# Decoder layer: expert_w applied to the latents in the feed-forward part instead of to fc2_w, and x2's transposes moved up in stage one's end

## The reference, cut to what matters

```
x = layernorm(x + attention(x, Wq, Wk, Wv))                 # 1024 tokens x 1024
x = layernorm(x + fake_quant(x) @ fake_quant(ctx))          # "cross"
# feed-forward, hidden = x
logits = hidden @ gate_w                                     # 8 experts
r      = sum(top_k(logits, 2))                               # one number a token
shared = relu(hidden @ up_w) ** 2 @ down_w                   # 1024 -> 2048 -> 1024
latent = hidden @ fc1_w                                      # 1024 -> 512
routed = ((latent @ expert_w) * r) @ fc2_w                   # 512 -> 512 -> 1024
x = layernorm(x + layernorm(shared + routed, ln_gamma, ln_beta))
```

## Time and profile before

| | us |
|---|---|
| median of 3 runs | 710.58 (708.35 to 712.87) |
| the profiled execution | 706.96 |
| its span, first to last instruction | 705.2 |
| start of stage one's end (its last projected tile is done) to the last x2 store | 178.6 to 251.3 |
| feature products | 262.1 to 490.3 |
| phases | 493.4 to the norms' end at 705 |

### The profile page before, as it was taken

The page is one execution under the profiler, slowest core; times in us unless marked ns, Lnnn a source line. Parts: engine busy times, 40 slices in busy tenths (PEclk is TensorE's granted clock), DMA queues, the critical chain, the costliest instruction groups (busy, mean ns, idle before and its releaser), DMA issues.

```text
span 705.2 us, 7841 instructions
## 1 busy us (share of the span) xinstructions
PE 620.1 (88%) x2952; PEld 501.4 (71%) x2960; DVE 415.0 (59%) x552; ACT 292.9 (42%) x378; POOL 137.9 (20%) x162
## 2 busy tenths in 40 slices
PE   4598699887559879989999999998999999999972
PEld 3487577765348548868888888886888888888862
DVE  6846788997888523222334222132875555769976
ACT  4545555556363524222233323203254433434825
POOL 3424283555730411313110000000000000000000
PEclk9999999998878999999999999999999999999987
DMA  9654335433761469684884825500433235352402
GB/s 337 226 170 152 112 108 169 131 92 102 244 198 39 145 203 316 207 293 149 263 304 149 273 107 158 171 8 1 122 113 94 89 91 201 126 210 61 148 31 119
DMA packets 80887, 109.88 MB, mean 156 GB/s; under 512 B 23633, under 2 KB 54609, under 8 KB 80849
## 3 DMA queue, kind: packets, MB, share of 16 engines
q1 hardware_dynamic: 76096, 92.07, 40.6%
q0 software_dynamic: 2448, 8.91, 3.6%
q10 hardware_dynamic: 2304, 8.39, 3.5%
HBM read 79.99 MB, written 25.17 MB: 149 GB/s over the span
## 4 chain that ended last, share of the span: by engine, by line
PE 58%; DVE 21%; DMA 7%; issue 5%; ACT 4%; SPq 4%; POOL 2%; POOLq 0%; DVEq 0%; ACTq 0%
PE acc_b L1172 31%; PE acc_a L1201 13%; PE acc_b L1201 8%; DMA c_sb<-in_ctx_dram 2%; SPq L243 1%; SPq L235 1%; DVE stat L571 1%; DMA x_scratch<-res 1%; PE qkv_ps L283 1%; PE sc_ps L300 1%; DVE o_sb L615 1%; ACT y_sb L425 1%; DVE x2T_hi L1457 1%; PE xa_ps L325 1%; DVE stat_n L1508 1%
## 5 line engine op out<-in xcount | busy, mean ns | idle before, releaser
L1388 DVE TENSOR_TENSOR u_lo<-u_raw,u_hi 128x1024 fp32r<-128x1024 f32 x18 | 23.3, 1293 | 123.1 <-ACT u_hi L1244 123.1
L1172 PE MATMUL acc_b<-x2T_hi,u_hi 128*128 128x512 f32 x160 | 63.3, 396 | 0.0
L1172 PE MATMUL acc_b<-x1T_hi,u_hi 128*128 128x512 f32 x160 | 62.4, 390 | 0.0
L1172 PE MATMUL acc_b<-x2T_hi,u_lo 128*128 128x512 f32 x160 | 62.4, 390 | 0.0
L1172 PE MATMUL acc_b<-x2T_lo,u_hi 128*128 128x512 f32 x160 | 62.3, 390 | 0.0
L1172 PE MATMUL acc_b<-x1T_hi,u_lo 128*128 128x512 f32 x160 | 62.3, 389 | 0.0
L1172 PE MATMUL acc_b<-x1T_lo,u_hi 128*128 128x512 f32 x160 | 62.3, 389 | 0.0
L283 PE MATMUL qkv_ps<-w_hi,xT_hi 128*128 128x512 f32 (+1 forms) x128 | 35.9, 362 | 14.7 <-DVE w_lo L642 10.0
L1201 PE MATMUL acc_a<-x2T_lo,x2T_hi 128*128 128x512 f32 x168 | 41.8, 404 | 3.8 <-DVE x2T_lo L1459 3.8
L1201 PE MATMUL acc_a<-x1T_hi,x2T_hi 128*128 128x512 f32 x168 | 41.1, 399 | 3.0 <-DVE x1T_hi L1459 3.0
L1201 PEld LDWEIGHTS acc_a<-x2T_lo,x2T_hi 128*128 128x128 f32 x168 | 32.9, 197 | 11.7 <-issue 4.6
(11 more groups left out here) (235 smaller groups left out, 1346.1 us busy)
## 6 DMA issues: line engine op xcount, KB each, us to landing
d_raw<-in_L_ffn_down_w_dram SPq DMA_DIRECT2D x28, 512.0 KB, 5.5
t_scratch<-d_raw SPq DMA_DIRECT2D x20, 512.0 KB, 4.2
d_raw<-t_scratch SPq DMA_DIRECT2D x20, 512.0 KB, 3.8
c_sb<-in_ctx_dram ACTq DMA_DIRECT2D x16, 512.0 KB, 4.7
u_raw<-in_L_ffn_up_w_dram SPq DMA_DIRECT2D x16, 512.0 KB, 6.6
x_sb<-in_x_dram SPq DMA_DIRECT2D x8, 512.0 KB, 4.7
res<-in_x_dram SPq DMA_DIRECT2D x8, 512.0 KB, 3.4
x_scratch<-res SPq DMA_DIRECT2D x8, 512.0 KB, 3.6
```

The source lines that it names most:

```text
L1172: mm = pe.matmul(acc_b[:, q % 4], s, v, start=(k == 0 and i == 0), stop=(k == KT - 1 and i == 2))
L1388: dve.tensor_tensor(u_lo[:, m % 2], u_raw[:, m % 2], u_hi[:, m % 2].bitcast(F32), ALU.subtract).then_inc(S["u_lo_done"], 1)
```

## The change

- expert_w is no longer multiplied by fc2_w. All of the w2 work of stage one goes: loads, transposes, splits, the 8 products, copies, stores, the scratch.
- Part two makes the latents first (4 blocks of fc1_w by 2 batches). ACT and DVE split each product into high and low parts. expert_w is loaded by SP behind the column loads and gamma, and split. Eight expert products (expert_product, 4 row blocks by 2 batches, 4 x 3 matmuls each) follow, and DVE multiplies them by rT. Then come the 16 up blocks. The last pair of feature blocks in the phases is the expert output, and its rows of the second operand are fc2_w itself.
- The routing and spreading steps come earlier, between the latent products. down_w's sums follow another timetable (SUMS_AT), with their stores two blocks later. rT, gamma, beta, ones and r_diag get storage of their own; the features are laid out in three parts each.
- In stage one x2's column blocks get eight buffers instead of four, all eight are loaded in step 8, and all eight transposes stand in PE's list in step 8: 0 and 1 ahead of values(6), 2 to 7 behind it and ahead of scores(7). On DVE x2T_lo 0 to 3 stand ahead of first_stats(5), 4 and 5 ahead of normalise(5), 6 and 7 ahead of collect(6). On ACT softmax_exp(7) stands ahead of q1T_out(5).
- The first two weight blocks that stage one loads and splits are of fc1_w.
- Code for making some up products already in stage one (early_product and its like) is there but off: EARLY = 0.

The diff, cut to its core:

```diff
+EARLY = 0
...
-                if k >= 4:
-                    sp.wait_ge(S["x2T_ready"], k - 3)
-                sp.dma_start(xk[k % 4], x2_dram[0:SEQ, k * P:(k + 1) * P].rearrange("(t p) c -> p t c", p=P)).then_inc(xk_in[k % 4], 16)
+                    sp.wait_ge(S["c_done"], BATCH * CK)
+                sp.dma_start(xk[k], x2_dram[0:SEQ, k * P:(k + 1) * P].rearrange("(t p) c -> p t c", p=P)).then_inc(xk_in[k], 16)
...
-                if s == TILES - 1:
-
-                    sp.wait_ge(S["scores_ready"], TILES - 1)
-                    for l in range(MT):
-                        sp.dma_start(ex_raw[l], args["expert_w"][l * P:(l + 1) * P, :]).then_inc(ex_in, 16)
-                    sp.wait_ge(S["xT_ready"], TILES)
-                    sp.wait_ge(S["c_done"], BATCH * CK)
-                    for m in range(MT):
-                        sp.dma_start(fc2_raw[m], args["fc2_w"][m * P:(m + 1) * P, :]).then_inc(fc2_in[m], 16)
-                if s == TILES + 3:
-                    store_w2(range(MT - 1))
...
                 if s == TILES:
-                    transpose_expert(0)
-                    transpose_expert(1)
-                if s == TILES + 1:
-                    transpose_x2(4)
-                    transpose_x2(5)
+                    transpose_x2(0)
+                    transpose_x2(1)
                 if in_range(s - 2):
                     values(s - 2)
                 if s == TILES:
-                    transpose_expert(2)
-                    transpose_expert(3)
-                    transpose_x2(0)
-                    transpose_x2(1)
-                if s == TILES + 1:
-                    transpose_x2(6)
-                    transpose_x2(7)
+                    for k in range(2, KT):
+                        transpose_x2(k)
...
-                for q in w2_ahead.get(s, ()):
-                    w2_product(q)
...
                 if s == TILES + 1:
-                    fc2_lo_out(0)
-                    fc2_lo_out(1)
                     softmax_transpose(s - 2)
-                    x2T_lo_out(4)
-                    x2T_lo_out(5)
-                    fc2_lo_out(2)
-                    fc2_lo_out(3)
                     collect(s - 2)
-                    x2T_lo_out(6)
-                    x2T_lo_out(7)
...
                 if s == TILES:
                     softmax_transpose(s - 2)
-                if s == TILES:
-                    expert_lo(0)
-                    expert_lo(1)
+                    for k in range(4):
+                        x2T_lo_out(k)
                 if s in (TILES, TILES + 1):
                     first_stats(s - 3)
...
+                if s == TILES:
+                    x2T_lo_out(4)
+                    x2T_lo_out(5)
...
                 if s == TILES:
+                    x2T_lo_out(6)
+                    x2T_lo_out(7)
                     collect(s - 2)
...
+            def expert_product(e, b):
+
+                q = expert_index(e, b)
+                bank_free(q)
+                pe.wait_ge(S["ex_lo_done"], 2)
+                for l in range(MT):
+                    pe.wait_ge(S["lat_lo_done"], latent_index(l, b) + 1)
+                    st = [x[:, l, e * P:(e + 1) * P] for x in (ex_hi, ex_lo)]
+                    for i, (s, v) in enumerate(split_products(st, [lat[l][b][:, h] for h in range(2)])):
+                        mm = pe.matmul(acc_b[:, q % 4], s, v, start=(l == 0 and i == 0), stop=(l == MT - 1 and i == 2))
                 mm.then_inc(S["op_used"], 1)
...
             routing(0)
+            latent_product(0, 0)
+            transpose_logits(0)
+            latent_product(1, 0)
+            latent_product(0, 1)
+            spread_r(0)
+            latent_product(1, 1)
+            routing(1)
+            latent_product(2, 0)
+            transpose_logits(1)
+            latent_product(2, 1)
+            latent_product(3, 0)
+            spread_r(1)
+            latent_product(3, 1)
             for b in range(BATCH):
-                for m in range(2):
-                    product(m, b)
-                    if (m, b) == (0, 0):
-                        transpose_logits(0)
-            for m in range(2, MU):
-                for b in range(BATCH):
-                    product(m, b)
-                if m == 2:
-                    spread_r(0)
-                if m == 3:
-                    routing(1)
-                if m == 4:
-                    transpose_logits(1)
-                if m == 6:
-                    spread_r(1)
+                for e in range(MT):
+                    expert_product(e, b)
+            for m in range(MU):
+                if m >= EARLY:
+                    up_product(m, 0)
+                up_product(m, 1)
```

More of the change, by code:

```diff
@@ L91, in attention_and_cross @@
         q1T = sb("q1T", [P, 2, KT, P], BF16)
[L92 to L95, removed]
+        q2 = sb("q2", [P, BATCH, CK, EMB], BF16)
         c_sb = sb("c_sb", [P, 2, EMB], F32)
@@ L753, in _ @@
                     magic(s - 3)
+                    for m in range(5, min(6, EARLY)):
+                        early_lo(m)
                 if in_range(s - 4):
@@ L940, in feed_forward, with two_types, h_pair, h_slot @@
         xT_hi, xT_lo = [so["x2T_hi"], x1_hi], [so["x2T_lo"], x1_lo]
-        f1b0, f2b0, f1b1, f2b1 = [sb(n, [P, NP, SEQ], F32) for n in ("f1b0", "f2b0", "f1b1", "f2b1")]
-        h_block = lambda m, b: ((f1b0, f1b1), (f2b0, f2b1))[m % 2][b][:, m // 2]
+        def two_types(name, slots):
+            with nc.sbuf_tensor(name + "_r", [P, slots, SEQ], F32R) as rounded:
+                pass
+            return rounded, sb(name, [P, slots, SEQ], F32)
+        ex_hi, h_a1 = two_types("h_a1", 4)
+        ex_lo, h_a2 = two_types("h_a2", 4)
+        lat_st, h_b = zip(*[two_types(f"h_b{i}", 4) for i in range(4)])
+        h_c = [sb(f"h_c{i}", [P, 2, SEQ], F32) for i in range(4)]
+        part_of = [(so["hx1"][:, KT:KT + 4], h_b[0], h_c[0]), (so["hx2"][:, KT:KT + 4], h_b[1], h_c[1]), (h_a1, h_b[2], h_c[2]), (h_a2, h_b[3], h_c[3])]
+        def h_pair(half, b, j):
+            part = part_of[2 * b + half][j // 2]
+            return part[:, 2 * (j % 2):2 * (j % 2) + 2]
+        def h_slot(half, b, k):
+            return h_pair(half, b, k // 2)[:, k % 2]
+        lat = [[lat_st[2 * b + l // 2][:, 2 * (l % 2):2 * (l % 2) + 2] for b in range(BATCH)] for l in range(MT)]
         s3_own = sb("s3_own", [P, 2, SEQ], F32)
@@ L989, in feed_forward, with u_src @@
         up_cols, fc1_cols = [args[w].rearrange("(k p) (m c) -> m p k c", p=P, c=P) for w in ("up_w", "fc1_w")]
-        def u_src(m):
-            half, j = m % 2, m // 2
-            return up_cols[half * UP + j] if j < UP else fc1_cols[half * (NP - UP) + j - UP]
+        def u_src(w):
+            return fc1_cols[w] if w < MT else up_cols[(w - MT) % 2 * UP + (w - MT) // 2]
         def d_rows(half, k, tiles=1):
             return args["down_w"][(half * UP + k) * P:(half * UP + k + tiles) * P] if k < UP else \
-                w2_dram[(half * (NP - UP) + k - UP) * P:(half * (NP - UP) + k - UP + tiles) * P]
+                args["fc2_w"][(half * (NP - UP) + k - UP) * P:(half * (NP - UP) + k - UP + tiles) * P]
         t_rows = lambda half, k, tiles=1: t_dram[half][k * P:(k + tiles) * P, :]
@@ L1026, in a_raw @@
         def a_raw(phase, j):
-            return s3_of(j) if phase == "p7" else pair({"p1": f1b0, "p6": f1b0, "p5": f1b1, "p4": f2b1, "p3": f1b0, "p2": f2b0}[phase], j)
+            return s3_of(j) if phase == "p7" else h_pair(*{"p1": (0, 0), "p6": (0, 0), "p5": (0, 1), "p4": (1, 1), "p3": (0, 0), "p2": (1, 0)}[phase], j)
         def consumed(eng, s):
```

462 lines of the change are left out of this document (256 added, 206 removed).

## The result

| | before | after |
|---|---|---|
| median, the four runs of each made together, us | 709.47 (706.85 to 712.87) | 729.79 (729.32 to 731.50) |
| ratio | | 1.0288, 95% interval 1.0238 to 1.0338 |
| the profiled execution; its span | 706.96; 705.2 | 731.5; 729.7 |
| TensorE's first matmul of part two | 253.62 | 259.45 |
| start of p1 | 493.40 | 520.26 |

Differences between profiles are therefore read stage by stage here. Three points of TensorE's own list cut the 24.5 us into stages: part two starts 5.8 us later, the stretch from there to p1 is 21.0 us longer (260.8 against 239.8), and what follows p1's start is 2.4 us shorter (209.4 against 211.8).

A forecast was written before the change was run, and what follows sets the result against it. TensorE was taken to bound the feature products, a chain through all engines stage one's end. +21.8 - 2.6 + 1.7 + 2.0 = +22.9 us, from the median 710.58 giving 733.5; forecast 733, range 722 to 741.

The forecast's parts named there:

- The matmuls, +21.8: Feature products: 96 added expert matmuls at 0.227 us each, with nothing to cover them, lengthen the kernel by 21.8 us.
- the wait for rT, -2.6: Feature products: TensorE's 2.63 us idle before the routing of batch 1 goes, -2.6 us.
- The start of p1, +1.7: Hand-over from feature products to p1: TensorE's wait grows from 3.14 to 4.8 us, +1.7.
- Stage one's end, +2.0: End of stage one: earlier loads offset by moved transposes, then slow-clock crosses; both halves together +2.0 us.
- The first half: Stage one's end up to normalise(6): moved transposes take what the dropped split gave, +0.2 us, normalise(6) near 225.2.
- the clock of cross(7): Second half of stage one's end: slow clock after idle TensorE, 1.9 us charged for this cross, likewise for cross(6).
- The second half: Stage one's end from normalise(6) to part two's opening: clock charges less two small gains, sum +2.3 us.
- The term for values(7): First half of stage one's end: values(7) follows cross(5) closely and takes 2.0 us instead of 3.78, gaining 1.8.
- 0.8 off for transpose_q1(7): Second half of stage one's end: this transpose no longer stands behind the w2 products, -0.8 us.
- The 0.7 for the landing: Opening of part two: the last landing is x2's at 254.9, not w2's at 255.6, -0.7 us.
- stage one's end becomes clearly shorter: Rival on stage one's end: 9 us come off through less VectorE work and earlier transposes, 722 us; chance 0.13.
- PE's clock stays low: Rival on stage one's end: crosses 5, 6, 7 each 3.4 us dearer, +29 in all, 740 us; chance 0.12.

The follow-up runs named there:

- experiment 1: Kernel before with each of the 8 w2 products cut from 12 matmuls to 1: 712.45 us, ratio to before 1.0023.
- 2: Kernel after with each of the 8 expert products cut from 12 matmuls to 1: 716.81 us, ratio to before 1.0116.
- experiment 4: Kernel after with p1's first three high parts ahead of the last relu on ScalarE: 724.11 us, ratio to before 1.0201.
- experiment 9: Kernel before with the low parts of p1's first pair ahead of the last latent on VectorE: 702.83 us, ratio to before 0.9921.
- experiment 3: Kernel after with x2's transposes and splits in the order of before, early loads and eight buffers kept: 723.97 us, ratio to before 1.0207.
- run 7: Kernel after with x2's order of before, p1's first splits early and filler matmuls (40, 12 and 24): 712.95 us, ratio to before 1.0086.
- 10: Kernel after with x2's order of before and p1's first splits early, no filler matmuls: 718.50 us, ratio to before 1.0124.
- 5: Kernel after with 102 filler matmuls that feed nothing in TensorE's pauses of stage one's end: 728.57 us, ratio to before 1.0282.
- 8: Kernel after with EARLY = 8 and p1's first splits ahead of the last relu: 725.97 us, ratio to before 1.0247.
- 6: Kernel after with EARLY = 8, eight up products made in stage one: 734.48 us, ratio to before 1.0359.
- run 11: Kernel before with p1's first low parts moved up and p3's last low parts ahead of four tiles' statistics: 702.68 us, ratio to before 0.9910.

## Why the prediction was right, and where its terms were off

733 was forecast with 722 to 741, and slower with 0.94; 729.8 came. +22.9 was predicted; the medians give +20.3, the profiles +24.5. That 729.8 lies so near 733 is in part luck: stage one's end was taken 3.8 us too short, and a tail that came out 2.4 us shorter by chance made up for most of it. Stage by stage, profile against profile:

- **The matmuls, +21.8, and the wait for rT, -2.6: right.** Together +19.2 against the measured +19.4. Experiments 1 and 2 show both sides: 20 us of w2 matmuls were worth nothing where they lay, the expert matmuls are on the path where they are. Inside the 19.4 are small terms that I had not listed. Part two now opens at the low clock: its 16 routing matmuls need 2.4 us more (6.1 against 3.7), behind a pause of 7.70 us where before, with the last w2 product behind cross(7), it was 2.77. The wait of before for the loads of x2's second batch, 1.3 us, is gone. With them the sum makes 20.3; the 0.9 us by which the stretch is shorter than that I can't place.
- **The start of p1, +1.7: right.** The wait is 4.78 us, +1.6; experiment 4 removes it and finds the place of all of it in ScalarE's list. I did not say what experiment 9 shows, that the 3.14 us of before were a loss of 5 us to be had by moving two instructions.
- **Stage one's end, +2.0: the mechanism right, the size not.** It is +5.8. The first half (+2.4 and not +0.2) and the clock of cross(7) (+2.8 and not +1.9) were mis-sized. The second half as a whole came to +3.5, where I had +2.3, and laying both halves out together had taken another 0.5 off.
  - In the first half I put softmax_max(7) at 206.4; it is 208.3. I took the column loads as 1.04 us apart, and the second came 2.1 us behind the first. I also took scores(7) with 2.9 us; it stands behind a pause of 5.37 us and took 3.75. My +0.2 is +2.4 (normalise(6) at 227.37, forecast 225.2). The term for values(7) held: 1.95 us, forecast 2.0.
  - In the second half I charged 1.9 us of low clock for each cross. cross(6) lost 1.8 (5.46 against 3.63), but cross(7) lost 2.8. The 1.9 came from p1's burst of 24 matmuls, whose clock came back within the burst; behind cross(6) TensorE paused again for 4.43 us, and in cross(7) the clock came back later.
  - I took 0.8 off for transpose_q1(7), and that held: before, it started 0.9 us behind its input (239.06, 239.97), now 0.06 (243.49, 243.55). The 0.7 for the landing is 0.5 up to TensorE's first matmul of part two (257.59 to 259.45, before 251.30 to 253.62). The loads behind the last store start 1.7 us sooner after it (2.7 against 4.4), but that first matmul doesn't wait for them; they count in the next stage, as the 1.3 us of wait that is gone there. In all 2.4 + 1.8 + 2.8 - 0.8 - 0.5 = 5.7, of 5.8 measured.
- **The tail, which I took as unchanged, is 2.4 us shorter**, by chance and not by the change (below).

The rival "stage one's end becomes clearly shorter" asked the right question: the end could have been shorter. With the transposes left where they were, part two starts 6.8 us earlier than in after (experiment 3), and with fillers as well 12.5 us earlier (run 7, 246.90 against 259.45). The moved transposes took the gain away, as the sum said. The rival "PE's clock stays low" was half true: the slow level held cross(5) as well, 5.63 us where it had been at the full clock. Little of these 2.0 us came through, since values(7) gave back 1.8 behind it. The Trainium skill ("Perfetto Trace Analysis", Matmul Optimizations) advises back-to-back matmuls because the engine's power follows its use. The trace agrees in the direction: 0.70 against 0.88 as the clock of the stretch, with 37.5 against 55.0 us of TensorE's work in it.

From the kernel after, by the ratios to before, experiments take off 5.7 us (the order, 3), 6.2 (the start of p1, 4) and 2.7 (the pauses left empty, 10 against 7; by itself not clear of noise, 4.7 in the traces), and at run 7 some 6 us to the kernel before are left. By the profiled executions of run 7 and before these are +18.4 for the feature products without the wait at their end (255.0 against 236.6), -6.7 for the earlier start of part two, and the 3.1 of wait, 1.7 of slow start and 1.1 of tail that run 7 is spared. Since the hand-over to p1 can be mended in the kernel before as well (run 9), the like comparison is run 7 with run 9, 1.0086 with 0.9921: the change costs 1.7%, some 12 us (8 to 15), even with its side effects mended.

What stays open: how much of the 4.7 and 5.9 us that the fillers gave at the start of part two (7 against 10, and 5) reaches the time of the whole kernel, which the intervals of 5 us and more don't tell; and the 0.9 us above.

## What to carry to other kernels

An operation's cost is set by where it stands: 96 matmuls in the gaps of a chain bound by other engines cost nothing, the same 96 in a stretch where TensorE is full cost 21.8 us, and taking them back out of there would return only what the next engine's own chain leaves (12 to 13 of 20 us). Before work is moved up in an in-order list, ask what stands behind it: eight transposes ahead of scores(7) made the chain wait for work that nobody needed until part two. And look at the hand-over between stages first; moving one pair of low parts ahead of one multiply gave 5.4 us and was the edit that beat the kernel before.

## What the runs showed that was not expected

**Empty gaps cost TensorE's clock, and so the work behind them.** Removing matmuls that were off the path made those on the path slower: cross(7) took 3.63 us with the w2 products ahead of it, 6.30 without them (experiment 1), 6.46 in the kernel after, and 3.63 again with fillers (5 and 7). Where the time of a kernel has several us of spread, such an effect is seen sooner in the length of a stage between two points of the same list than in the median of four runs.

**The same wait is not always followed by the low level.** Ahead of p3's last group TensorE waits 3.0 us in 12 of the 13 traces, always for the same low part. In six of them (before and runs 3, 5, 7, 8, 9) the matmuls behind it fall to the 1.2 GHz level for a while; in the six others (after and runs 1, 2, 4, 6, 10) they don't. TensorE's timeline and the clock of 4 us there, before and then after (in after the wait takes the first half of the 4 us):

```profile
676.03 2.90 PE L1201 MATMUL acc_a<-x1T_hi,x2T_hi 128*128 128x512 f32 x6 [3.01 <-DVE x1T_hi L1459]
...
678.00:682.00 4.00, 4.00 (x11) 3.11 (x10) 2.92 (x5) 0.29 (x1) 0.00 (x0) 0.52 0.00 0
```

```profile
702.92 1.62 PE L1233 MATMUL acc_a<-x1T_hi,x2T_hi 128*128 128x512 f32 x6 [3.02 <-DVE x1T_hi L1519]
...
701.00:705.00 4.00, 2.08 (x9) 1.76 (x10) 2.19 (x3) 0.00 (x0) 0.00 (x0) 1.00 0.00 0
```

From the first of these matmuls to the 25th it took 8.28 us before and 5.56 in the kernel after. These 2.7 us cover the 2.4 by which the tail differs, and as far as the traces tell they belong to neither kernel: at such a wait a term of up to 2.7 us comes or doesn't come. The waits of 3.75 and 3.62 us in runs 6 and 8 show the same. Where the wait was 0.73 us (run 11, one trace) the level held.
